# Outputs and statistics by batch element, and other rearrangements, in a four-layer decoder kernel

## Chip, cores and metric

The kernel runs on one core of one Trainium2 chip. The metric is the device time of one launch in microseconds (us), the median of several runs. The engines are TensorE (PE, its weight loads PEld), VectorE (DVE), ScalarE (ACT), GpSimd (POOL) and SyncE (SP), which issues most DMAs.

## The reference

Two sequences of 512 tokens with 128 features pass twelve residual stages, each on its layer norm:

```python
for f in (L0_attn, L0_xattn, L0_ffn, L1_attn, L1_xattn, L1_ffn,
          L2_attn, L2_xattn, L2_ffn, L3_attn, L3_xattn, L3_ffn):
    x = x + f(layernorm(x), ...)
```

The parts that matter here:

- `L0_attn` and `L1_attn` are causal attentions of 16 heads, `L2_attn` is a full one; each ends in an output projection, `out = o @ Wo`.
- `L1_xattn` takes its queries from x, and its keys and values from x and from a context of 77 tokens, with 2 heads.
- `L2_xattn` and `L3_xattn` are cross attentions of 16 narrow heads (8 features each) onto the 77 context tokens. `L2_xattn` clips its scores to 10000, and an output whose softmax sums are not numbers is replaced by an average.
- `L2_ffn` is a mixture of 16 experts with an RMS norm of its own, which has a weight: `xn = xf / rms * norm_weight; logits = xn @ router_weight.T + router_bias`. Each expert takes its 64 best tokens, `xe = xn[idx]`.

## The kernel before

The whole activation `m.x` stays in SBUF as 8 tiles of 128 tokens: tiles 0 to 3 are batch element 0 ("half 0"), 4 to 7 are element 1 ("half 1"). Each stage (l0a, l0x, l0f, l1a, l1x, l1f, l2a, l2x, l2f, l3a, l3x, l3f) has a function for every engine. Each engine issues its instructions in the order in which they are written, stage after stage, with semaphore waits between the engines.

**PSUM banks.** There are eight. A named result (`item`) has a bank: `fill` makes TensorE wait until all earlier results of that bank have been taken out, `read` makes a reader wait until the result is there, `copied` until it is taken out. `pair` and `run` in `plan` give bank 6 to the even numbers of a list and bank 7 to the odd ones. So `l1xo0`, `l1xy0`, `l2ao0`, `l2ay0` are in bank 6, and `l1xo1`, `l1xy1`, `l2ao1`, `l2ay1` in bank 7. In l2x the small results `l2xg0` and `l2xh0` are in bank 6, and so is `l2xy0`. The attention results of l0a and l1a are in bank 7.

**End of an attention stage.** TensorE writes x (the identity times x, `x_tensor`, one matmul of 128x512 a half) into the two y banks and adds the output projection (`tokens_tensor` or `sums_tensor`, four token tiles a half; in l1a four terms a tile). A float32 matmul shows as two instructions in the trace. VectorE takes the statistics of each half from the bank (`moments_of_sums`, `half_moments`: bn_stats, bn_aggr, variance). GpSimd makes the root (`norm_gpsimd`), ScalarE copies the new x out (`take_x`), VectorE normalises each half (`norm_to_turn`), TensorE turns it (`turn_tensor`), and ScalarE copies the turned tokens (`turn_scalar`, L223). Meanwhile TensorE issues fillers, matmuls of the identity with itself whose result nobody reads (`busy_through_norm`): so many, a wait for both variances, so many, a wait for the first root, so many. The attention result gets into `o_t` through GpSimd in l0a and l1a (`quad_scaled` counts its halves or groups), through ScalarE in l1x and l2a, through VectorE in l2x and l3x. At the start of l3f, GpSimd clears two buffers after l3x's statistics and before it makes the roots.

**The narrow loops** (l2x and l3x, `narrow_cross` and `narrow_vector`). There are 16 steps: batch element, query tile, half of the heads. TensorE issues in step k the scores of step k (L1950, into banks 0 and 1 or 2 and 3); the transposes of step k-3 (L1964, into banks 4 and 5), which wait for the exponential and for ScalarE's copy of the transposes before (`cross_taken`); and in every second step, for steps k-6 and k-5 together, the values (L1977) and the sums (L1982) into one bank. VectorE does in step k, in l2x, clip and maximum, in l3x maximum and subtraction; and in every second step, a step after TensorE's sums, the reciprocal group (L1901 and following: reciprocal of the sums, output times it, in l2x also a sum over the reciprocals). In l2x GpSimd subtracts the maximum (L2080). ScalarE does the exponential of step k (L897) and the copy of the transposes of step k-2 (L913).

**l2f's norm.** VectorE makes (x - mean) times the norm weight, a row repeated on all partitions, and then multiplies by the root. TensorE turns the tiles, ScalarE copies them. After the routing a matmul gathers the chosen tokens and ScalarE copies them (`chosen_t`, L2226).

Of the kernel before, what the change touches and what calls it, by code (L numbers as in the profile page):

```python
# [598 lines left out]
def l0_attn_tensor(nc, pe, m):  # L599
# [43 lines left out]
    x_tensor(nc, pe, m, "l0y")  # L643
    pe.wait_ge(m.quad_scaled, B)
    tokens_tensor(nc, pe, m, "l0y", m.o_t, w["wo"], on_x=True)


# [7 lines left out]
def x_tensor(nc, pe, m, name):  # L655


    for j in range(2):
        bank = fill(m, pe, f"{name}{j}")
        nc.tensor.matmul(bank[:, :], m.ident[:, :], m.x[:, 4 * j:4 * j + 4, :].rearrange("p t d -> p (t d)"), start=True,  # L660
                         stop=False, skip_group_check=True)


def tokens_tensor(nc, pe, m, name, x_t, w, on_x=False):
    sums_tensor(nc, pe, m, name, [(lambda t: x_t[:, t * P:(t + 1) * P], w)], on_x)


def sums_tensor(nc, pe, m, name, pairs, on_x):

    for j in range(2):  # L670
# [8 lines left out]
def project_out_tensor(nc, pe, m, source, name, w):  # L679

    x_tensor(nc, pe, m, name)
    for j in range(2):
        copied(m, pe, f"{source}{j}")
    tokens_tensor(nc, pe, m, name, m.o_t, w, on_x=True)
# [688 lines left out]
def l1_attn_tensor(nc, pe, m):  # L1373
# [51 lines left out]
    def q_ready(pe, b, j, qt):  # L1425
        group = GROUP * b + j
        if qt == 0 and group >= EARLY:
# [10 lines left out]
    x_tensor(nc, pe, m, "l1az")  # L1438
    pe.wait_ge(m.quad_scaled, B + 2 * GROUP)
    sums_tensor(nc, pe, m, "l1az", [(lambda t, r=r: m.wide[:, r, t * P:(t + 1) * P], m.lat_out[:, r * P:(r + 1) * P])  # L1440
                                    for r in range(GROUP)], on_x=True)

# [80 lines left out]
def l1_cross_tensor(nc, pe, m):  # L1523
# [34 lines left out]
    for k in range(XSTEPS + 3):  # L1558
# [20 lines left out]
        if j >= 0 and (j + 1) % (2 * NQ) == 0:  # L1579
            b = j // (2 * NQ)  # L1580
            pe.wait_ge(m.cross_taken, x0 + j + 1)
# [13 lines left out]
    project_out_tensor(nc, pe, m, "l1xo", "l1xy", w["wo"])  # L1595


def l1_cross_scalar(nc, act, m):
# [46 lines left out]
    copy_out_scalar(nc, act, m, "l1xo", m.o_t)  # L1645
# [156 lines left out]
def l2_attn_tensor(nc, pe, m):  # L1802
# [29 lines left out]
    project_out_tensor(nc, pe, m, "l2ao", "l2ay", w["wo"])  # L1832
# [44 lines left out]
def narrow_vector(nc, dve, m, a, stage):  # L1877
# [3 lines left out]
    for k in range(XSTEPS + 6):  # L1881
# [14 lines left out]
        n = k - 6  # L1896
# [10 lines left out]
def narrow_cross(stage, clip=None):  # L1907
# [8 lines left out]
    def tensor(nc, pe, m):  # L1916
# [24 lines left out]
        for k in range(XSTEPS + 5):  # L1941
# [26 lines left out]
            if n >= 0 and n % 2 == 1:  # L1968
# [6 lines left out]
                for j in range(GROUP):  # L1975
                    for g in range(GROUP):
                        nc.tensor.matmul(bank[own(g), 0:P], m.values_own[0:SC, b, g, j, :],  # L1977
                                         m.xpt[0:SC, g % 2, g // 2 * GROUP + j, qt * P:(qt + 1) * P], start=j == 0, stop=False,
                                         skip_group_check=True)
                for j in range(GROUP):  # L1980
# [5 lines left out]
        if clip:  # L1986
# [11 lines left out]
            keep_busy(nc, m, 7, 0)  # L1998
            pe.wait_ge(m.sums_are_numbers, 3)
        x_tensor(nc, pe, m, f"{stage}y")  # L2000
        copied(m, pe, f"{stage}o{B * NQ - 2}")
        copied(m, pe, f"{stage}o{B * NQ - 1}")
        tokens_tensor(nc, pe, m, f"{stage}y", m.o_t, w["wo"], on_x=True)
# [207 lines left out]
def l2_ffn_scalar(nc, act, m):  # L2211
# [3 lines left out]
    turn_scalar(nc, act, m, "l2fn")  # L2215
# [1611 lines left out]
```

## Time and profile before

| | |
|---|---|
| median of 3 runs | 1432.03 us (1428.06 to 1438.11) |
| profiled execution | 1430.51 us, its span 1428.7 us |
| mean granted TensorE clock | 0.979 |
| busy PE, DVE, ACT, POOL | 1333.0, 929.2, 671.9, 345.4 us |
| chain that ended last | PE 75%, DVE 11%, ACT 5%, DMA 4%, issue 3%, POOL 1% |
| first x product at the end of l0a, l1a, l1x, l2a | 136.50, 484.51, 566.71, 628.65 us |
| first x product at the end of l2x, l3x | 703.22, 911.23 us |

A time in the trace counts from the start of the span. In a timeline, a line is a run of like instructions: start us, length us from the first start to the last end, engine, line of the kernel, operation, output from inputs, form and count; in brackets the idle time of the engine before it and what ended that. A clock of 1.00 is 2.4 GHz, 0.50 is 1.2 GHz. Matmuls are pipelined, so that consecutive lines of TensorE can overlap by some 0.1 us.

### The profile page before, as it was taken

Reading aid. Unit: us, or ns where it says so; the run is one execution under the profiler, and the core shown is the slowest. Engines: PE = TensorE matmul, PEld = TensorE weight load, DVE = VectorE, ACT = ScalarE, POOL = GpSimd, SP = SyncE. Lnnn points to the kernel's source line nnn. Section 1 sums busy time; section 2 is a strip of 40 time slices with the busy share of each in tenths; the row PEclk is TensorE's granted clock in tenths of the full one; section 3 lists DMA queues with packets and bytes.
Section 4 is the critical chain, followed back from the end, with each engine's and each line's share of the span. In section 5 each row is a group of like instructions: output and inputs, shape, how many; then the busy total and the mean of one; then the engine's idle time right before and its main releaser. Section 6 shows DMA issues by size and latency. Waiting matters only on the chain.

```text
span 1428.7 us, 29436 instructions
## 1 busy us (share of the span) xinstructions
PE 1333.0 (93%) x11626; PEld 861.1 (60%) x11626; DVE 929.2 (65%) x1890; ACT 671.9 (47%) x1697; POOL 345.4 (24%) x373
## 2 busy tenths in 40 slices
PE   8998999999999889999989898899999999999986
PEld 6766565446666765667868586754435555654434
DVE  6776765343667555356684367588888876678755
ACT  5886533342787454344303245425557777740002
POOL 4000330001011100114203011177787465300001
PEclk9999999999999999999999989999999999999998
DMA  3000105100000000000124002101020110699980
GB/s 135 3 2 3 40 0 202 52 29 16 2 2 3 18 1 0 21 4 2 46 99 134 12 7 82 31 16 45 30 59 16 22 26 16 142 220 253 248 198 15
DMA packets 25352, 80.60 MB, mean 56 GB/s; under 512 B 5243, under 2 KB 7306, under 8 KB 24834
## 3 DMA queue, kind: packets, MB, share of 16 engines
q1 hardware_dynamic: 24354, 75.60, 19.4%
q10 hardware_dynamic: 864, 3.15, 0.8%
q8 instruction: 92, 1.51, 0.4%
q14 instruction: 42, 0.34, 0.1%
HBM read 72.17 MB, written 1.08 MB: 51 GB/s over the span
## 4 chain that ended last, share of the span: by engine, by line
PE 75%; DVE 11%; ACT 5%; DMA 4%; issue 3%; POOL 1%; SPq 0%; DVEq 0%; ACTq 0%; POOLq 0%
PE psum L2967 7%; PE psum L196 7%; PE psum L431 5%; PE psum L2988 5%; PE psum L2681 4%; PE psum L1267 4%; PE psum L2637 4%; PE psum L1261 3%; PE psum L451 3%; PE psum L2651 3%; PE psum L495 2%; PE psum L674 2%; DMA heads<-scratch_out_gates 2%; PE psum L2690 2%; DMA context_v<-scratch_out_gates 2%
## 5 line engine op out<-in xcount | busy, mean ns | idle before, releaser
L196 PE MATMUL psum<-ident 128*128 128x128 f32 x1272 | 159.6, 284 | 9.1 <-DMA ident<-in_ident 3.8
L187 POOL TENSOR_TENSOR rstd<-var,minus_half 128x4 f32<-128x4 f32 x30 | 31.3, 1043 | 557.9 <-DVE var L144 528.4
L196 PEld LDWEIGHTS psum<-ident 128*128 128x128 f32 x1272 | 153.2, 199 | 17.1 <-issue 7.7
L574 DVE TENSOR_REDUCE quad_max<-psum 128x1 f32<-128x128 f32 (+3 forms) x256 | 113.1, 484 | 55.8 <-PE psum L435 53.9
L529 ACT ACTIVATE pt<-psum,quad_max 128x128 f32<-128x128 f32 (+3 forms) x256 | 133.3, 530 | 26.7 <-DVE quad_max L574 26.6
L2988 PE MATMUL psum<-pt,slots 128*128 128x512 f32 x256 | 114.6, 599 | 5.0 <-DVE pt L3142 4.7
L2967 PE MATMUL psum<-slots,xn_t 128*128 128x512 f32 x256 | 113.9, 605 | 3.1 <-DVEq L3113 3.1
L2726 ACT ACTIVATE p<-psum,duo_max 128x512 f32<-128x512 f32 x128 | 86.8, 683 | 41.8 <-DVE duo_max L2761 41.7
L3057 ACT ACTIVATE pt<-psum,p 128x64 f32<-128x64 f32 x256 | 57.8, 392 | 72.7 <-POOL wide L3199 41.9
L2988 PEld LDWEIGHTS psum<-pt,slots 128*128 128x128 f32 x256 | 47.1, 189 | 71.7 <-issue 48.8
L2967 PEld LDWEIGHTS psum<-slots,xn_t 128*128 128x128 f32 x256 | 49.6, 194 | 66.0 <-issue 57.8
L2761 DVE TENSOR_REDUCE duo_max<-psum 128x1 f32<-128x512 f32 x128 | 82.3, 684 | 10.1 <-PE psum L2637 8.0
L2681 PEld LDWEIGHTS psum<-pt,wide 128*64 128x64 f32 x1024 | 54.6, 136 | 47.8 <-issue 25.0
L1349 DVE TENSOR_TENSOR pt<-pt,wide 128x512 f32<-128x512 f32 x64 | 43.0, 690 | 52.5 <-ACT pt L1296 43.0
L3130 DVE TENSOR_TENSOR pt<-psum,p 128x512 f32<-128x512 f32 x96 | 65.3, 686 | 17.8 <-PE psum L2967 13.5
L957 ACT ACTIVATE o_t<-psum 128x512 f32<-128x512 f32 x12 | 6.9, 596 | 142.7 <-PE psum L651 118.5
L2637 PE MATMUL psum<-heads 64*128 64x512 f32 x256 | 70.4, 630 | 3.2 <-ACT pt L3057 3.2
L2681 PE MATMUL psum<-pt,wide 128*64 128x128 f32 x1024 | 69.9, 279 | 1.1 <-ACT wide L2717 1.1
L451 PE MATMUL psum<-ident,pt 64*128 64x64 f32 x1280 | 63.8, 229 | 7.5 <-DVE pt L511 3.1
L1296 ACT ACTIVATE pt<-psum,slots 128x512 f32<-128x512 f32 x64 | 44.0, 687 | 56.5 <-PE psum L1261 56.3
L2709 DVE COPY pt<-psum 128x512 f32<-128x512 f32 x64 | 44.2, 691 | 40.0 <-PE psum L2651 39.4
L511 DVE COPY pt<-psum 128x256 f32<-128x256 f32 (+1 forms) x96 | 57.0, 593 | 10.7 <-PE psum L451 10.1
(515 smaller groups left out, 2796.8 us busy)
## 6 DMA issues: line engine op xcount, KB each, us to landing
pt<-scratch_out_gates SPq DMA_DIRECT2D x32, 256.0 KB, 12.9
heads<-scratch_out_gates SPq DMA_DIRECT2D x24, 256.0 KB, 15.6
slots<-in_s_l0f SPq DMA_DIRECT2D x8, 514.0 KB, 3.3
wide<-scratch_gates SPq DMA_DIRECT2D x8, 512.0 KB, 6.9
slots<-in_s_l3v SPq DMA_DIRECT2D x8, 512.0 KB, 3.7
context_v<-scratch_out_gates SPq DMA_DIRECT2D x16, 256.0 KB, 18.1
slots<-in_s_l3o ACTq DMA_DIRECT2D x6, 512.0 KB, 10.3
weights<-in_w_l1a SPq DMA_DIRECT2D x1, 2624.0 KB, 9.7
```

The lines of the kernel that those rows point to most:

```text
L196: nc.tensor.matmul(m.ps[bank][:, 0:P], m.ident[:, :], m.ident[:, :], start=True, stop=True, skip_group_check=True)
L431: nc.tensor.matmul(m.ps[g][:, 0:keys], q(g, b, j, qt), k(g, b, keys), start=True, stop=False)
L451: last = nc.tensor.transpose(banks[half][:, at:at + 64], m.quad_p[own, n % 2, g, kt * P:(kt + 1) * P], m.ident[own, own])
L529: nc.scalar.activation(m.quad_p[:, i % 2, g, 0:keys], m.ps[g][:, 0:keys], ACT.Exp, bias=m.quad_max[:, i % 2, g:g + 1], accum_out=sum_colum ...
L574: nc.vector.tensor_reduce(m.quad_max[:, n % 2, g:g + 1], m.ps[g][:, 0:keys], AX.X, ALU.max, negate=True).then_inc(m.quad_negmax, 1)
L2637: nc.tensor.matmul(m.ps[2 * (n % 2) + e], m.pair_rope[own, r % 2, 0, b * S + qt * P:b * S + (qt + 1) * P], m.pair_rope[own, r % 2, 1, b * ...
L2681: last = nc.tensor.matmul(m.ps[O_BANK][64 * e:64 * e + 64, qt * P:(qt + 1) * P], m.wide[:, r, at:at + 64], m.duo_pt[:, n % 2, e, kt * P:(k ...
L2726: nc.scalar.activation(m.p[:, 2 * (i % 2) + e, :], m.ps[2 * (i % 2) + e], ACT.Exp, bias=m.duo_max[:, i % 2, e:e + 1], accum_out=m.quad_sum ...
L2761: nc.vector.tensor_reduce(m.duo_max[:, n % 2, e:e + 1], m.ps[2 * (n % 2) + e], AX.X, ALU.max, negate=True).then_inc(m.duo_negmax, 1)
L2967: nc.tensor.matmul(m.ps[n % MIX_BANKS], m.xn_t[:, t * P:(t + 1) * P], m.slots[:, pair % 2, h * S:(h + 1) * S], start=True, stop=True).then ...
L2988: nc.tensor.matmul(m.ps[6 + b], m.slots[:, r % 2, e * P:(e + 1) * P], m.gated[:, k % 4, :], start=False, stop=False, skip_group_check=True ...
L3130: tt(by_feature(mixed[:, n % 4, :]), by_feature(m.ps[n % MIX_BANKS]), gate.rearrange("p (o e) -> p o e", o=1).broadcast_to([P, 64, E3]), A ...
```

## The change

- In l0a, l1a, l1x, l2a and l3x the x product and the projection are issued for half 0 and then for half 1, each behind its own wait. In l1x half 0 goes ahead of the attention values of batch element 1, and ScalarE copies the first half of `o_t` within its loop.
- In the loops of l2x and l3x the sums are issued one step after the values, behind that step's scores and transposes; VectorE's reciprocal group goes a step later too.
- At the end of l2x the x products take the place of the last seven fillers, ahead of the wait for VectorE's masked copy.
- In l2f the norm weight is a column and becomes the scale of ScalarE's copies of the turned and of the chosen tokens; VectorE normalises as in the other stages.

The diff, without most of its context lines:

```diff
@@ -640,9 +640,10 @@
     pe.wait_ge(m.quad_taken[T_BANKS.index(6)], a.turns_end[T_BANKS.index(6)])
-    x_tensor(nc, pe, m, "l0y")
-    pe.wait_ge(m.quad_scaled, B)
-    tokens_tensor(nc, pe, m, "l0y", m.o_t, w["wo"], on_x=True)
+    for j in range(2):
+        x_tensor(nc, pe, m, "l0y", (j,))
+        pe.wait_ge(m.quad_scaled, j + 1)
+        tokens_tensor(nc, pe, m, "l0y", m.o_t, w["wo"], on_x=True, halves=(j,))
@@ -652,22 +653,22 @@
-def x_tensor(nc, pe, m, name):
-    for j in range(2):
+def x_tensor(nc, pe, m, name, halves=range(2)):
+    for j in halves:
         bank = fill(m, pe, f"{name}{j}")
-def tokens_tensor(nc, pe, m, name, x_t, w, on_x=False):
-    sums_tensor(nc, pe, m, name, [(lambda t: x_t[:, t * P:(t + 1) * P], w)], on_x)
-def sums_tensor(nc, pe, m, name, pairs, on_x):
-    for j in range(2):
+def tokens_tensor(nc, pe, m, name, x_t, w, on_x=False, halves=range(2)):
+    sums_tensor(nc, pe, m, name, [(lambda t: x_t[:, t * P:(t + 1) * P], w)], on_x, halves)
+def sums_tensor(nc, pe, m, name, pairs, on_x, halves=range(2)):
+    for j in halves:
         bank = m.ps[m.items[f"{name}{j}"][0]] if on_x else fill(m, pe, f"{name}{j}")
@@ -676,12 +677,12 @@
-def project_out_tensor(nc, pe, m, source, name, w):
-    x_tensor(nc, pe, m, name)
-    for j in range(2):
-        copied(m, pe, f"{source}{j}")
-    tokens_tensor(nc, pe, m, name, m.o_t, w, on_x=True)
+def project_out_half(nc, pe, m, source, name, w, j):
+    x_tensor(nc, pe, m, name, (j,))
+    copied(m, pe, f"{source}{j}")
+    tokens_tensor(nc, pe, m, name, m.o_t, w, on_x=True, halves=(j,))
@@ -1435,10 +1436,11 @@
     pe.wait_ge(m.quad_taken[T_BANKS.index(6)], a.turns_end[T_BANKS.index(6)])
-    x_tensor(nc, pe, m, "l1az")
-    pe.wait_ge(m.quad_scaled, B + 2 * GROUP)
-    sums_tensor(nc, pe, m, "l1az", [(lambda t, r=r: m.wide[:, r, t * P:(t + 1) * P], m.lat_out[:, r * P:(r + 1) * P])
-                                    for r in range(GROUP)], on_x=True)
+    for j in range(2):
+        x_tensor(nc, pe, m, "l1az", (j,))
+        pe.wait_ge(m.quad_scaled, B + (j + 1) * GROUP)
+        sums_tensor(nc, pe, m, "l1az", [(lambda t, r=r: m.wide[:, r, t * P:(t + 1) * P], m.lat_out[:, r * P:(r + 1) * P])
+                                        for r in range(GROUP)], on_x=True, halves=(j,))
@@ -1578,6 +1580,8 @@
             b = j // (2 * NQ)
+            if b == 1:
+                project_out_half(nc, pe, m, "l1xo", "l1xy", w["wo"], 0)
             pe.wait_ge(m.cross_taken, x0 + j + 1)
@@ -1592,7 +1596,7 @@
             last.then_inc(filled(m, f"l1xo{b}"), 1)
-    project_out_tensor(nc, pe, m, "l1xo", "l1xy", w["wo"])
+    project_out_half(nc, pe, m, "l1xo", "l1xy", w["wo"], 1)
@@ -1642,7 +1646,10 @@
                                  turned_of(m, j).rearrange("p (b q) -> p b q", q=P), ACT.Copy).then_inc(m.cross_taken, 1)
-    copy_out_scalar(nc, act, m, "l1xo", m.o_t)
+        if k in (2 * NQ + 5, XSTEPS + 1):
+            b = 0 if k < XSTEPS else 1
+            bank = read(m, act, f"l1xo{b}")
+            nc.scalar.activation(m.o_t[:, b * S:(b + 1) * S], bank[:, :], ACT.Copy).then_inc(emptied(m, f"l1xo{b}"), 1)
@@ -1829,7 +1836,8 @@
     attend_tensor(nc, pe, m, None, a)
-    project_out_tensor(nc, pe, m, "l2ao", "l2ay", w["wo"])
+    for j in range(2):
+        project_out_half(nc, pe, m, "l2ao", "l2ay", w["wo"], j)
@@ -1878,7 +1886,7 @@
     nk, d = a.nk, m.dve
-    for k in range(XSTEPS + 6):
+    for k in range(XSTEPS + 7):
         if k < XSTEPS:
@@ -1893,7 +1901,7 @@
                 nc.vector.tensor_tensor(to, scores, spread, ALU.subtract).then_inc(m.negmax_ready, 1)
-        n = k - 6
+        n = k - 7
         if n >= 0 and n % 2 == 1:
@@ -1938,7 +1946,7 @@
         own = lambda g: slice(32 * g, 32 * g + 32)
-        for k in range(XSTEPS + 5):
+        for k in range(XSTEPS + 6):
             if k < XSTEPS:
@@ -1977,6 +1985,11 @@
                                          skip_group_check=True)
+            n = k - 6
+            if n >= 0 and n % 2 == 1:
+                b, _, qt = units[n]
+                name = f"{stage}o{n // 2}"
+                bank = m.ps[m.items[name][0]]
                 for j in range(GROUP):
@@ -1995,12 +2008,14 @@
                              stop=True).then_inc(filled(m, f"{stage}h0"), 1)
-            keep_busy(nc, m, 7, 0)
+            x_tensor(nc, pe, m, f"{stage}y")
             pe.wait_ge(m.sums_are_numbers, 3)
-        x_tensor(nc, pe, m, f"{stage}y")
-        copied(m, pe, f"{stage}o{B * NQ - 2}")
-        copied(m, pe, f"{stage}o{B * NQ - 1}")
-        tokens_tensor(nc, pe, m, f"{stage}y", m.o_t, w["wo"], on_x=True)
+            tokens_tensor(nc, pe, m, f"{stage}y", m.o_t, w["wo"], on_x=True)
+        else:
+            for j in range(2):
+                x_tensor(nc, pe, m, f"{stage}y", (j,))
+                copied(m, pe, f"{stage}o{B * NQ - 2 + j}")
+                tokens_tensor(nc, pe, m, f"{stage}y", m.o_t, w["wo"], on_x=True, halves=(j,))
@@ -2212,7 +2227,7 @@
     take_x(nc, act, m, "l2xy", 11)
-    turn_scalar(nc, act, m, "l2fn")
+    turn_scalar(nc, act, m, "l2fn", scale=w["norm_w"])
     bank = read(m, act, "l2fr0")
@@ -2223,7 +2238,8 @@
         bank = read(m, act, f"l2fx{j}")
-        nc.scalar.activation(m.chosen_t[:, j * S:(j + 1) * S], bank, ACT.Copy).then_inc(emptied(m, f"l2fx{j}"), 1)
+        nc.scalar.activation(m.chosen_t[:, j * S:(j + 1) * S], bank, ACT.Copy, scale=w["norm_w"]).then_inc(
+            emptied(m, f"l2fx{j}"), 1)
@@ -2245,16 +2261,7 @@
     dve.wait_ge(m.loaded["l2f"], 16)
-    for j in range(2):
-        copied(m, dve, f"l2xy{j}")
-        last = less_mean_times(nc, m, lambda t: m.x[:, t, :], w["norm_w"], j)
-    d.done(last)
-    for j in range(2):
-        root_of_half(dve, m)
-        for t in range(4 * j, 4 * j + 4):
-            last = nc.vector.tensor_scalar(m.xn[:, t, :], m.xn[:, t, :], m.rstd[:, t:t + 1], None, ALU.mult)
-        last.then_inc(m.xn_ready, 1)
-    m.turns_dve += 2
+    norm_to_turn(nc, dve, m, sums="l2xy")
@@ -3721,7 +3728,7 @@
                     ("router_b", column(np.tile(np.pad(v["L2_ffn_router_bias"], (0, 32 - E2)), 4))),
-                    ("norm_w", every(v["L2_ffn_norm_weight"])),
+                    ("norm_w", v["L2_ffn_norm_weight"].reshape(P, 1)),
                     ("one_to_cap", every(np.arange(1, CAP + 1, dtype=np.float32)))]
```

## Rows read from the trace of the kernel before

**Rows 1.** Timeline of TensorE, end of l0a.

```profile
136.50 1.88 PE L660 MATMUL psum<-x,ident 128*128 128x512 f32 x4
138.78 2.05 PE L674 MATMUL psum<-weights,o_t 128*128 128x128 f32 x16 [0.41 <-POOL o_t L561]
```

**Rows 2.** Timelines of TensorE and VectorE, end of l1a.

```profile
493.48 5.75 PE L196 MATMUL psum<-ident 128*128 128x128 f32 x50
...
495.26 2.38 DVE L161 TENSOR_SCALAR xn<-x,moments,rstd 128x128 f32<-128x128 f32 x8
```

**Rows 3.** Timelines of TensorE and ScalarE, end of l1x.

```profile
562.26 3.65 PE L1588 MATMUL psum<-pt,v 128*64 128x512 f32 x16 [0.69 <-ACT pt L1643]
...
566.71 1.98 PE L660 MATMUL psum<-x,ident 128*128 128x512 f32 x4
...
576.37 0.66 PE L215 MATMUL psum<-ident,xn 128*128 128x128 f32 x4 [0.37 <-DVE xn L161]
...
566.82 0.60 ACT L957 ACTIVATE o_t<-psum 128x512 f32<-128x512 f32 x1 [4.12 <-PE psum L1591]
```

**Rows 4.** Timeline of TensorE, end of l2a.

```profile
628.65 1.02 PE L660 MATMUL psum<-x,ident 128*128 128x512 f32 x2
629.98 1.12 PE L660 MATMUL psum<-x,ident 128*128 128x512 f32 x2 [0.30 <-ACT o_t L1854]
```

**Rows 5.** Chain in order of time, loop of l2x: start, length, what.

```profile
677.09 0.77 PE psum L1964 x16
677.86 1.01 PE psum L1977 x32
678.87 0.87 PE psum L1982 x32
679.74 0.74 PE psum L1950 x4
...
682.14 0.88 DVE k_t L1901
```

**Rows 6.** Windows, loop of l2x: busy PE, PEld, DVE, ACT, POOL; clock.

```profile
670.30:677.10 6.80, 6.74 (x90) 5.06 (x82) 3.19 (x5) 2.73 (x4) 1.69 (x2) 0.50 0.01 2
...
682.50:688.10 5.60, 3.91 (x100) 3.36 (x100) 4.54 (x8) 3.26 (x5) 2.44 (x3) 1.00 0.01 3
```

**Rows 7.** Timeline of TensorE, loop of l2x, transposes.

```profile
669.37 0.77 PE L1964 MATMUL psum<-ident,p 64*77 64x64 f32 x16 [1.59 <-ACT pt L913]
...
688.28 0.77 PE L1964 MATMUL psum<-ident,p 64*77 64x64 f32 x16 [1.69 <-ACT pt L913]
```

**Rows 8.** Timelines of TensorE and VectorE, end of l2x.

```profile
703.22 1.98 PE L660 MATMUL psum<-x,ident 128*128 128x512 f32 x4
...
701.81 1.35 DVE L2058 COPY_PREDICATED o_t<-number,average 128x512 f32<-128x512 uint32 x2
```

**Rows 9.** Timeline of TensorE, start of l2f, fillers.

```profile
706.82 6.86 PE L196 MATMUL psum<-ident 128*128 128x128 f32 x60
```

**Rows 10.** Line L223 on ScalarE by form: count, min/median/max ns.

```profile
L223 ACT ACTIVATE xn_t<-psum x24: 592/597/598, 11.5 to 1401.6; 128x512 f32<-128x512 f32 x24
L223 ACT ACTIVATE xn_t<-psum,weights x4: 682/729/777, 146.1 to 500.4; 128x512 f32<-128x512 f32 x4
```

**Rows 11.** Timeline of TensorE, loop and end of l3x.

```profile
876.79 0.77 PE L1964 MATMUL psum<-ident,p 64*77 64x64 f32 x16 [0.63 <-ACT pt L913]
...
902.35 0.77 PE L1964 MATMUL psum<-ident,p 64*77 64x64 f32 x16 [1.20 <-ACT pt L913]
...
912.70 1.12 PE L660 MATMUL psum<-x,ident 128*128 128x512 f32 x2 [0.35 <-DVE o_t L1902]
```

**Rows 12.** Chain in order of time, loop and end of l3x.

```profile
885.27 0.56 PE psum L1964 x16
...
914.75 0.90 DVE stats L134 x4
...
917.60 0.96 POOL v L3175
```

## The prediction

> **What bounds the kernel now.** I read the page first. TensorE carries 75% of the chain that ended last (the table of the profile above), so a change pays only where it shortens TensorE's own order of work, or where TensorE stands idle. The change touches six stage ends and two loops. For each I read the timeline of TensorE, to see its idle time and what ended it; then the timelines of VectorE, ScalarE and GpSimd; then the chain in order of time. The reader is to see that the ends differ. Some have short idle gaps on TensorE; at the end of l1a fillers run on after the result that they bridge to is there [rows 2]. In the two narrow loops TensorE waits in every pair of steps for ScalarE's copy, itself the end of a chain in l2x and alone in l3x [rows 7, 11].
>
> **Unit costs.** An x product of one half (identity times x) is half of the 1.88 us row: 0.94. The eight matmul instructions of one half's projection are about 0.9: sixteen end 2.05 after the start, pipeline fill included [rows 1]. VectorE's statistics take 1.4 us a half: both halves run from 914.75 to just before 917.60 [rows 12].
>
> **End of l0a.** Now: both x products, an idle 0.41 for GpSimd's second scaling, then sixteen projection instructions up to 140.83 [rows 1]. Changed: x0 to 137.44, projection 0 to 138.33, x1 to 139.27. The scaling is over by 138.78, so projection 1 ends near 140.2. The weight folds queued behind it on TensorE start 0.6 earlier. VectorE's and GpSimd's earlier statistics lie beside these folds and give nothing more. Gain 0.6 (0.3 to 0.7).
>
> **End of l1a.** The wait for the scaling is over long before the sums, and the same TensorE work follows in another order. The second half's sums end when they did. Behind them stand 25 fillers (50 instructions) from 493.48 to 499.2, while the normalised tokens are ready at 497.64 [rows 2]. First statistics that come 1 us earlier meet fillers that run by count. Gain 0 (up to 0.2).
>
> **End of l1x.** The first half's x product and projection (0.94 + 0.9) move ahead of the second values, into the 0.69 us in which TensorE waits for ScalarE. So the values start at 563.3 and not at 562.26, and end 1.05 later, at 567.8. Their consumer, ScalarE's copy, also comes 1.05 later. Now the trap: the second output's bank, 7, is also that of the second attention result (both lists alternate 6 and 7). The x product of half 1 must therefore wait for this copy of 0.60, which today ends under the x product of half 0 [rows 3]. It starts at about 568.5, takes 1.1 after an idle wait, and projection 1 ends at 570.5, as today. The old gap is filled and a new one of the same size appears. What is left: today statistics 1 queue 0.5 behind statistics 0 (1.4, begun when half 0's projection ends, 0.9 before half 1's); this queue goes. Behind the projection 22 fillers run by count; only the 0.37 us wait ahead of the second turn goes [rows 3]. Gain 0.3 (0 to 1.1, the latter without the trap). ScalarE's first o_t copy moves into the loop, where ScalarE waits for VectorE's maxima; that covers it. If that cover were gone, it would cost its own 0.60 [rows 3].
>
> **End of l2a.** Today x1 starts at 629.98, after 0.30 idle for the copy of the second attention result [rows 4]. Changed: x0 to 629.6, projection 0 to 630.5, and x1 starts there, the copy being over. Projection 1 ends at 632.35 instead of 632.88. Gain 0.5 (0.3 to 0.6).
>
> **The loop of l2x.** A step pair in full clock takes 11.19 / 2 = 5.6 us: 677.09 to 688.28 is four steps [rows 5, 7]. The chain through these four: transposes, values 1.01, sums 0.87, scores 0.74 on TensorE, VectorE's clip and maximum, the reciprocal group (0.88 and on, about 1.4), clip and maximum again, GpSimd, exponential, copy, transposes. The change takes both the sums (0.87) and the reciprocal group (1.4) out of this chain, each behind the next scores. Without them it would be 8.9 for four steps, 4.5 a pair. But VectorE's own work of a pair is 4.54 [rows 6], and its order, with the copy-before-transposes rule of a single pair of banks, leaves some waiting. I take halfway between 5.6 and 4.6: 5.1 a pair, over six pairs (0.5 each): 2.9 (0.5 to 6). The result bank is not reused for three more steps, so neither the fill of that bank nor the in-order reciprocal waits for anything new.
>
> One stretch of this loop ran at 0.50 granted clock, that is 1.2 GHz, from 670.3 to 677.1, right after an idle 1.59 us on TensorE. The pair there took 7.72 instead of 5.6 (669.37 to 677.09), so it costs 2.1 [rows 5 to 7]. With shorter waits I expect no such stretch here: 2.1 more (0 to 2.1). The Trainium skill ("TensorE: Matmul & The Clock Gate", Part 1) says that the gate looks at activity without regard to where a kernel starts, so that the same kernel differs from run to run. By that, the runs of before need not all have had this stretch here and the 2.1 would be partly noise; the trace of one execution cannot show it.
>
> **End of l2x.** Seven fillers give way to the x products, which then need not run behind the masked copy. Today the x products begin at 703.22. Changed: bank 6 is free only when VectorE has read the last small result in it, just before the masked copy starts at 701.81. So x0 starts near 701.9, x1 ends near 703.9, after the masked copy (703.16) [rows 8]. The projection starts 1.3 earlier than at 705.2. Gain 1.3 (1.2 to 1.8).
>
> **Norm weights in l2f.** VectorE loses eight scalar-tensor-tensor instructions and eight multiplies and gets eight fused ones. But TensorE runs 30 fillers (60 instructions, 6.86 us) by count in this interval [rows 9], and their number isn't changed, so VectorE's saving stays hidden. What costs is ScalarE's copy with a column of weights as scale: 729 ns against 597 [rows 10]. Of four such copies two end on the path: loss 0.2 (0 to 0.5). The Trainium skill ("ScalarE: Activation LUTs", What ACT_TABLE_LOAD costs) puts each such operand at about 93 ns; the row says 132, and the difference would be under 0.1 us in all. The smaller weight load ends ahead of need either way.
>
> **The loop of l3x.** Here TensorE waits 0.63 a pair for ScalarE's copy of the transposes just done. Five pairs take 25.56 us, 5.11 each [rows 11]. The chain of a pair: transposes 0.77, values 1.01, sums 0.87, scores 0.74 as in l2x [rows 5], second transposes 0.56 [rows 12], and the remaining 1.16 is the copy with its hand-overs. After the change sums and scores lie between the second transposes and the next ones, and they cover the copy. The pair becomes TensorE's own work: 0.56 + 1.01 + 0.74 + 0.56 + 1.0 (sums, now after transposes like the values) + 0.74 = 4.6. Gain 0.5 a pair, 2.6 for five; in the tail, where the wait is 1.20 [rows 11], 0.9 more. Gain 3.5 (1 to 4.3).
>
> **End of l3x.** x1 waits until 912.70 for VectorE's last o_t [rows 11], with projection 0 queued behind. Changed: projection 0 comes first and x1 starts at 913.1. Projection 1 ends 0.7 earlier; statistics 1 no longer queue behind statistics 0: 1.15 earlier. GpSimd's two memsets (from 917.60), the roots and the normalising all hang on that [rows 12], and here the fillers end before the roots. Gain 1.15 (0.7 to 1.4).
>
> **Sum.** 0.6 + 0 + 0.3 + 0.5 + 2.9 + 2.1 + 1.3 - 0.2 + 3.5 + 1.15 = 12.15. The profiled execution took 1430.51 (span 1428.7), 1.5 under the median of the runs, 1432.03. So 1418.4 for it and 1420 for the median, 0.8% less. A measurement of this kernel tells about 1% from no change, and three runs of before lie 10 us apart.
>
> **Rivals.** (A) The loops keep their pace where VectorE and GpSimd set it: l2x gives nothing, and its half-clock stretch stays; the rest stands. 12.15 - 2.9 - 2.1 = 7.2, so 1425. For it: VectorE has 4.54 of work in 5.6. Against: both removed terms lie in the chain itself. (B) The loops reach their floors: l2x at VectorE's 4.6 a pair (6.0 instead of 2.9), l3x without the extra 0.14 of sums after transposes (+0.8), and one more of the other half-clock stretches falls away (2.1). 12.15 + 6.0 = 18.2, so 1414. (C) The change does not do what it says: in-order engines hold the earlier halves back in both loops and ends, and only the replaced fillers and the end of l3x pay: 2.5, so 1430. Against it stand the named gaps. (D) Slower: TensorE's order with shorter matmul runs drops the clock inside the loops. A pair at half clock takes 7.7 [rows 5, 7] instead of 4.6 or 5.1. Four pairs at half clock cancel everything; all six of l3x make 18.6 of loss, 1439. Against: in l3x's loop with 0.63 us gaps the clock never fell, and the gaps shrink.
>
> **How the numbers follow.** Forecast 0.42, A 0.22, B 0.26, C 0.06, D 0.04. The range goes from 1411, below B with what run noise adds, to 1429, above A. Faster by over 1% (below 1417.7): B and the lower edge of the forecast, 0.36. Slower 0.03. Within 1%: 0.61.
>
> **What would show it.** L1982 a step after L1977; transposes of l3x's loop without idle time before them and 4.6 us a pair; l2x near 5.1 and at full clock; at the end of l1x an idle gap ahead of the second x product; the end of l1a and the l2f fillers unchanged in length; l3x's memsets 1.1 earlier relative to its last sums. I am wrong if transposes still wait in l3x, if the clock falls in either loop, or if half-clock stretches elsewhere outweigh all of it.

## The result, and the profile after

The changed kernel takes 1418.83 us (median of 7 runs, 1414.98 to 1423.37), the kernel before 1432.03 (also 7 runs, 1428.06 to 1438.11). The ratio is 0.991, with a 95% interval of 0.9888 to 0.9932: faster by 0.9%. The profiled execution took 1418.38 us (span 1416.6), against 1430.51 (span 1428.7): 12.1 less. I take the stages in the order of the prediction.

End of l0a, timeline of TensorE (start, length, engine, line, operation, idle time before it):

```profile
136.91 1.02 PE L661 MATMUL psum<-x,ident 128*128 128x512 f32 x2
137.77 1.05 PE L675 MATMUL psum<-weights,o_t 128*128 128x128 f32 x8
138.66 1.02 PE L661 MATMUL psum<-x,ident 128*128 128x512 f32 x2
139.52 1.05 PE L675 MATMUL psum<-weights,o_t 128*128 128x128 f32 x8
140.50 0.67 PE L1015 MATMUL psum<-keys_own,weights 64*128 64x156 f32 x6
```

The idle 0.41 ahead of the projection [rows 1] is gone. From the last transposes of the attention to the first weight fold it takes 4.03 us in place of 4.71. The end of l1a is unchanged (8.97 before and 8.96 after, from the first x product to the fillers).

End of l1x, the same view, and behind it a row of ScalarE's timeline:

```profile
561.96 1.02 PE L661 MATMUL psum<-x,ident 128*128 128x512 f32 x2
562.83 1.05 PE L675 MATMUL psum<-weights,o_t 128*128 128x128 f32 x8
563.81 3.65 PE L1592 MATMUL psum<-pt,v 128*64 128x512 f32 x16
...
569.02 1.12 PE L661 MATMUL psum<-x,ident 128*128 128x512 f32 x2 [0.70 <-ACT o_t L1652]
...
568.37 0.60 ACT L1652 ACTIVATE o_t<-psum 128x512 f32<-128x512 f32 x1 [5.61 <-PE psum L1595]
```

The first half fills the old wait of 0.69 ahead of the values [rows 3]. A new wait of 0.70 stands ahead of the second x product: it starts when ScalarE has emptied the bank. From the last transposes of l1x to l1f's own x product ("the end of l1x") it takes 15.21 us in place of 15.57. At the end of l2a the second x product starts at 630.63 without a wait; from the attention's last values to l2x's first product it takes 8.14 in place of 8.72.

Loop of l2x, from the chain in order of time (start, length, what):

```profile
675.42 0.77 PE psum L1972 x16
676.19 1.01 PE psum L1995 x32
677.20 0.74 PE psum L1958 x4
...
677.97 0.81 DVE p L1897
...
678.80 0.80 DVE xmax L1899
679.60 0.88 DVE k_t L1909
```

The sums (L1995, before L1982) now follow transposes, with no values in between. The reciprocal (k_t) still stands in the chain, between two pairs of VectorE's instructions. Four steps of this chain take 10.31 us (transposes at 665.11 to transposes at 675.42), before 11.19: what left it is one run of 0.87 on TensorE, not the group. The six pairs took 5.11, 6.07, 7.72, 5.60, 5.59 and 5.64 before, and 4.59, 5.00, 5.32, 4.99, 4.96 and 5.82 after.

The two loops as windows (start and end; length; busy time of PE, PEld, DVE, ACT, POOL; granted clock; DMA share; GB/s):

```profile
657.90:692.90 35.00, 33.09 (x774) 26.48 (x773) 24.81 (x40) 20.17 (x24) 13.26 (x13) 1.00 0.01 4
870.40:901.20 30.80, 29.99 (x756) 24.89 (x756) 23.25 (x34) 20.48 (x24) 0.00 (x0) 1.00 0.02 3
```

Both ran at clock 1.00 throughout, that is at 2.4 GHz, and TensorE is busy 95% and 97% of them. From the transposes ahead of the first values to the product behind the last sums, the loop of l2x takes 35.01 us in place of 40.06.

End of l2x and start of l2f, timelines of VectorE and TensorE:

```profile
696.42 1.34 DVE L2073 COPY_PREDICATED o_t<-number,average 128x512 f32<-128x512 uint32 x2
696.45 1.98 PE L661 MATMUL psum<-x,ident 128*128 128x512 f32 x4 [0.25 <-DVE number L2068]
698.27 1.95 PE L675 MATMUL psum<-weights,o_t 128*128 128x128 f32 x16
...
700.05 6.86 PE L196 MATMUL psum<-ident 128*128 128x128 f32 x60
...
702.35 2.38 DVE L161 TENSOR_SCALAR xn<-x,moments,rstd 128x128 f32<-128x128 f32 x8
```

The x products start beside the masked copy, when VectorE has read the last small result, and not behind it [rows 8]. The projection starts 5.41 us after the loop, before 6.79. In l2f the normalised tokens are ready at 704.73, but the fillers run until 706.75, as long as they did [rows 9]. From the projection to the router's matmul it takes 10.48 us, before 10.34.

Loop and end of l3x, the chain first, then timelines of TensorE and GpSimd:

```profile
872.85 0.54 PE psum L1972 x16
873.39 1.01 PE psum L1995 x32
874.40 0.72 PE psum L1958 x4
875.12 0.54 PE psum L1972 x16
875.66 1.01 PE psum L1985 x32
876.67 0.72 PE psum L1958 x4
```

```profile
901.25 1.13 PE L661 MATMUL psum<-x,ident 128*128 128x512 f32 x2
902.21 1.05 PE L675 MATMUL psum<-weights,o_t 128*128 128x128 f32 x8
...
906.49 0.96 POOL L3182 MEMSET v<- 128x1024 f32 x1 [48.43 <-DVEq L3637]
...
909.36 1.16 PE L196 MATMUL psum<-ident 128*128 128x128 f32 x8 [0.33 <-POOL rstd L187]
```

A pair is 4.54 us of TensorE's own work: two transposes, values, sums and two score groups, without the 0.63 of waiting [rows 11]. In the tail, where waits of 1.20 and 1.21 stood, transposes still wait 0.19, 0.43 and 0.19. The loop with its tail takes 30.90 us in place of 34.44 (from transposes at 870.35 to the x product at 901.25; before from the like ones to 911.23). From there to l3f's first product it takes 11.78 in place of 12.91.

The ledger: 0.68 + 0 + 0.36 + 0.58 + 5.05 + 1.38 - 0.14 + 3.54 + 1.13 = 12.58 us, against 12.1 less span. The six ends and the norm make 4.0 of it. Over the profiled kernels that share an end's code and run it at full clock, its length repeats within 0.05 us.

### The profile page after: what moved, and what is told of

Read it like the earlier page. It is cut to its first block, busy times and chain, and to the rows that moved or that the text cites. A ratio compares the mean times of both kernels' runs of the same rounds, so it can differ in the third digit from the quotient of the medians.

```text
span 1416.6 us, 29395 instructions
## 1 busy us (share of the span) xinstructions
PE 1330.0 (94%) x11612; PEld 860.1 (61%) x11612; DVE 927.6 (65%) x1882; ACT 672.1 (47%) x1697; POOL 344.6 (24%) x373
## 4 chain that ended last, share of the span: by engine, by line
PE 76%; DVE 11%; ACT 5%; DMA 4%; issue 3%; POOL 1%; SPq 0%; DVEq 0%; ACTq 0%; POOLq 0%
PE psum L2974 7%; PE psum L196 7%; PE psum L431 5%; PE psum L2995 5%; PE psum L2688 4%; PE psum L1268 4%; PE psum L2644 4%; PE psum L1262 3%; PE psum L451 3%; PE psum L2658 3%; PE psum L495 2%; PE psum L675 2%; PE psum L2697 2%; DMA heads<-scratch_out_gates 2%; DMA context_v<-scratch_out_gates 2%
## 5 line engine op out<-in xcount | busy, mean ns | idle before, releaser
L2995 PE MATMUL psum<-pt,slots 128*128 128x512 f32 x256 | 114.4, 598 | 4.7 <-DVE pt L3149 4.2
L2995 PEld LDWEIGHTS psum<-pt,slots 128*128 128x128 f32 x256 | 47.2, 189 | 71.1 <-issue 49.4
L2688 PEld LDWEIGHTS psum<-pt,wide 128*64 128x64 f32 x1024 | 54.6, 136 | 48.2 <-issue 24.3
```

The lines of the kernel that those rows point to most:

```text
L2688: last = nc.tensor.matmul(m.ps[O_BANK][64 * e:64 * e + 64, qt * P:(qt + 1) * P], m.wide[:, r, at:at + 64], m.duo_pt[:, n % 2, e, kt * P:(k ...
L2995: nc.tensor.matmul(m.ps[6 + b], m.slots[:, r % 2, e * P:(e + 1) * P], m.gated[:, k % 4, :], start=False, stop=False, skip_group_check=True ...
```

## The experiments

In each diff, "-" is the changed kernel and "+" the experiment, if not said otherwise. Kernels without a number of runs ran once, and their totals say little beside their stages: 1420.34 us (sums late only), 1427.09 (group late only), 1421.95 (own bank), 1420.23 (fewer fillers), 1413.19 (old norm, fewer fillers). Own bank and fewer fillers even came out above the changed kernel; both had 54.6 us at half clock ahead of the last 30, the changed kernel's profiled execution 47.8.

**The loops alone.** The kernel before, with only the sums and the reciprocal group a step later in the narrow crosses:

```
-    for k in range(XSTEPS + 6):        (VectorE)
+    for k in range(XSTEPS + 7):
-        n = k - 6
+        n = k - 7
-        for k in range(XSTEPS + 5):    (TensorE)
+        for k in range(XSTEPS + 6):
     ... the sums' matmuls moved under: n = k - 6; if n >= 0 and n % 2 == 1
```

> Only the later sums and the later reciprocal group, in both narrow loops, on the kernel before. My theory: from the first combined transposes on, l2x's loop takes 5.0 us less and l3x's 3.5 us less than before, all other stages take what they took; so 1430.5 - 8.5 = 1422 for the profiled execution, a ratio near 0.994. l3x's loop at 4.54 us a step pair without idle time before the transposes. Rival (the stage ends carry the gain): the loops give under 4 us together and the total stays above 1426.

Measured: 1420.66 us (6 runs), ratio 0.9927 (0.99 to 0.9955). l2x's loop took 35.01 and l3x's 30.9, as in the changed kernel; all ends kept their old times. In whole times the ends don't show clear of noise: 1418.83 us with them, 1420.66 without, and the intervals overlap. Their 4.0 us rest on the stages.

**All but the loops.** The changed kernel with the loops of before:

> The changed kernel with both narrow loops as they were. My theory: the stage ends give 0.7 (l0a), 0 (l1a), 0.4 (l1x), 0.6 (l2a), 1.4 (l2x), -0.1 (l2f) and 1.1 (l3x), 4 us together: 1426.5, ratio 0.997. Step pairs of 5.6 us in l2x and 5.11 in l3x. If the half-clock stretch in l2x's loop belongs to its idle time, it is there again; if it came there by the phase of the run alone, it is as likely elsewhere.

Measured: 1431.99 us (12 runs), ratio 0.9991 (0.9968 to 1.0014). The ends gained as in the changed kernel (l0a 4.07, l1x 15.22, l2a 8.14, l2x 5.42), but l3x's end took 12.95: a half-clock stretch from the loop reaches 2.4 us into it. And the loops lost: 42.93 and 36.6 us, against 40.06 and 34.44 before. The window in l2x's loop and the last of l3x, both at about half clock:

```profile
683.00:697.00 14.00, 12.80 (x156) 10.76 (x144) 4.39 (x8) 4.38 (x5) 3.54 (x5) 0.51 0.01 1
...
908.00:915.00 7.00, 7.00 (x101) 5.59 (x94) 2.50 (x4) 0.04 (x1) 0.00 (x0) 0.52 0.01 2
```

The expected 1426.5 us missed by 5.5. In this execution the ends' 2.8 us are in their stages, and the two loops, with their half-clock stretches, lost 5.0; this profiled execution (1432.81) lies 2.3 above the one before. This is one execution; that it also explains the median of twelve is argued, not shown. In its favour: the granted clock averages 0.979 over these runs and over the 39 runs of the kernel before that went with the timed experiments, and 0.984 for the loops alone.

**Which half of the loop edit.** Two kernels, each with one of its two moves: the sums on TensorE, or VectorE's reciprocal group.

```
sums late only                            group late only
-    for k in range(XSTEPS + 7):          -        for k in range(XSTEPS + 6):
+    for k in range(XSTEPS + 6):          +        for k in range(XSTEPS + 5):
-        n = k - 7                        and the sums' matmuls back under n = k - 5
+        n = k - 6
```

> TensorE's sums a step later as in the changed kernel, VectorE's reciprocal group back in its old step. My theory: l3x's loop, which waited for ScalarE's copy alone, keeps nearly all of its gain on TensorE's side, unless VectorE, which now must wait for sums that are issued in the same step behind the transposes, holds up the next maximum; VectorE then stands about 1 us a pair and the loop takes 4.6 to 5.2 a pair. In l2x, where VectorE is in the chain, the pair is slower than in the changed kernel's 5.1: 5.4 or more. Rival (moving the sums is all that counts): both loops as in the changed kernel.

> TensorE's sums back in their old step, VectorE's reciprocal group a step later. My theory: l3x's loop is back at 5.11 a pair, as its chain holds no VectorE work; in l2x the group (1.4) leaves the chain of four steps and the sums (0.87) stay: 11.19 - 1.4 = 9.8 for four steps, 4.9 to 5.3 a pair, against 5.6 before and 5.1 changed. Rival (both moves are needed together in l2x as well): 5.6 a pair.

Measured, sums alone: l3x 30.66 us with pairs of 4.54; l2x 35.61, 5.2 a pair on average and not the 5.4 or more of my theory. The old step of VectorE's group holds nothing up in l3x and costs 0.6 in all in l2x. Group alone: l2x 35.52 in pairs of 5.11, l3x in pairs of 5.11 as before, both as expected. TensorE's timeline in l3x, and a window of its tail, which ran at half clock, so that this loop took 37.36 us:

```profile
878.59 0.77 PE L1972 MATMUL psum<-ident,p 64*77 64x64 f32 x16 [0.63 <-ACT pt L914]
```

```profile
899.00:910.00 11.00, 11.00 (x147) 9.12 (x144) 2.94 (x7) 1.02 (x1) 0.00 (x0) 0.53 0.01 3
```

The wait of 0.63 is there again. In l3x only the place of the sums counts: they cover ScalarE's copy. In l2x either move takes some 2.4 us out of 38 (40.06 less the half-clock excess), and both together 3.0. The chain of l2x with the group alone tells why they don't add:

```profile
665.10 0.56 PE psum L1972 x16
...
665.68 1.03 ACT pt L914
...
666.84 0.77 PE psum L1972 x16
```

VectorE has left this chain. What is left is TensorE's work and the uncovered copy, as in l3x before, with the same 5.11 a pair. With the sums alone the copy is covered, but VectorE and its group stay in the chain. With both moves VectorE's group stands in the chain again, for the mean pair of 5.11. So the two kernels with the group late reach the same pair in l2x by two different limits.

**A bank of its own.** The second output product of l1x goes to bank 0, not to bank 7, which it shares with the second attention result:

```
+    if name == "l1xy1":
+        return m.ps[0]
     ... and the same bank wherever this result is read or added to
```

> The changed kernel with one edit: the x and weight products of l1xy1 go to bank 0, so they share no bank with l1xo1. Theory (the shared bank 7 made the second x product wait for ScalarE's copy): the 0.70 us wait before the second x product goes, TensorE runs the two x products, the first weight fold and the second without a gap but for the wait on ScalarE's copy of o_t ahead of the second weight products, and from the last transposes of l1x to the x product of l1f it takes between 14.5 (the whole 0.7 gained) and 15.2 us. Rival (the second weight products need the same copy a microsecond later, so the wait only moves behind the x product): the idle time shows there instead and the stage keeps its 15.21 us. By the rows, the copy ended when the second x product started, so after it the weight products find it done: I expect the gain, about 0.7 us. All other stages unchanged; the whole 1418.4 less 0.7 or so, within what one run can tell.

Measured, TensorE and ScalarE at the end of l1x:

```profile
569.02 1.03 PE L1601 MATMUL psum<-wide,context_v 77*64 77x512 f32 x4
...
569.98 1.12 PE L667 MATMUL psum<-x,ident 128*128 128x512 f32 x2
...
570.10 0.60 ACT L1658 ACTIVATE o_t<-psum 128x512 f32<-128x512 f32 x1 [5.61 <-PE psum L1601]
```

No wait is left on TensorE: the copy runs beside the x product. The end takes 14.45 us in place of 15.21, 0.76 less. The shared bank was the trap.

**Fewer fillers, with the new norm and with the old.** Three kernels: the fillers cut; the old two-step norm of l2f with the old fillers; the old norm with fewer fillers.

```
-    busy_through_norm(nc, pe, m, 6, 13, 8)          (into l1x)
+    busy_through_norm(nc, pe, m, 6, 13, 2, 3)
-    busy_through_norm(nc, pe, m, 11, 12, 8, 10)     (l2f)
+    busy_through_norm(nc, pe, m, 11, 12, 8, 1)
```

> The changed kernel with fewer of TensorE's counted 128-column filler matmuls under two norms: in l1x the last group 8 and 4 down to 2 and 3, in l2f 10 down to 1. Theory (behind the l2f norm VectorE ends 2.0 us ahead of the fillers, 704.73 against 706.75, and behind l1x's the fillers also run past the norm): the stretch from l2's projection to the router's matmul falls from 10.48 to about 8.5 us, l1x's end from 15.21 to about 13.8 us. Rival (the fillers hold nothing, another engine ends last): both keep their times and a wait shows in place of the fillers. A further risk: the granted clock falls to 0.50 in the stage behind, which would cost 3 to 7 us there.

> The changed kernel with the old VectorE norm of l2f (product with the weight row, then the product with the root) and plain ScalarE copies, everything else as changed. Theory (the saving on VectorE is hidden behind 60 filler matmuls and only the dearer scale copy shows): from the projection to the router's matmul 10.34 us, 0.13 less than the 10.48 of the changed kernel; whole 1418.3. Rival (the norm edit gave the gain that it was meant to and something else took it): 11 to 12 us here.

> The same old norm of l2f with the fewer filler matmuls of fewer_fillers. Theory: without the fillers' cover VectorE's two-step norm ends last in l2f, and the stretch from the projection to the router's matmul comes out at 9.7 us, against 8.5 with the new norm and the same fillers: so the norm edit is worth 1.2 us only if the fillers are cut with it. Rival (ScalarE's turn and copies set the end in both): both within 0.2 us of each other.

Measured from l2's projection to the router's matmul:

| | 30 fillers | 21 fillers |
|---|---|---|
| old norm | 10.35 | 9.46 |
| new norm (the change) | 10.48 | 8.47 |

The last waits, TensorE in the old norm with fewer fillers, and below it VectorE and TensorE with the new:

```profile
699.71 1.44 PE L215 MATMUL psum<-ident,xn 128*128 128x128 f32 x8 [0.56 <-DVE xn L2270]
```

```profile
703.91 2.38 DVE L161 TENSOR_SCALAR xn<-x,moments,rstd 128x128 f32<-128x128 f32 x8
...
706.30 1.04 PE L215 MATMUL psum<-ident,xn 128*128 128x128 f32 x8
```

So the new norm costs 0.13 us behind 30 fillers and saves 1.0 behind 21. The other cut lies ahead of l1x, between l1a's x product and l1x's turn (14.55 to 12.99); I had written "l1x's end", and the end stayed at 15.22. The granted clock was 1.00 in both shortened stretches. No run here shows how few fillers it would bear.

**The old norm, timed.** Its one execution above had taken 1413.59 us, 5.2 less than the changed kernel's median.

> The changed kernel with the old VectorE norm of l2f again, now timed. Its one execution took 1413.6 us, 5.2 less than the changed kernel, while its stages differ by only 0.13 us; the difference lay in where the half-clock stretches fell. If that was chance between executions (theory): median 1418 to 1419, ratio to the kernel before 0.991. If the old norm really is 5 us faster (rival): median 1413 to 1414, ratio 0.987.

Measured: 1416.93 us (6 runs, 1407.95 to 1421.48), ratio 0.9898 (0.9865 to 0.9932). It can't be told from the changed kernel's 0.991; the stages say 0.13 us. The first execution had 41 us at half clock ahead of its last 30, the profiled one of these six 47.8, with the very same code.

**GpSimd's roots first.** In l3f two memsets stood ahead of the roots:

```
     pool.wait_ge(m.stage_done, 11)
+    norm_gpsimd(nc, pool, m)
     for what in range(2):
         nc.gpsimd.memset(duo_turned_raw(m, what), 0.0).then_inc(m.turned_zero, 1)
-    norm_gpsimd(nc, pool, m)
```

> The changed kernel with GpSimd's two roots of l3f's norm put before its two memsets. Theory (with the statistics 1.8 us earlier, GpSimd's memsets at 906.49 and 907.39 now stand between the statistics and the roots; the roots start at 908.30): the roots run when the statistics come, the wait of 0.33 us for the roots and the one of 0.37 us for VectorE's norm go, and from the first x product after l3x's loop to l3f's first product it takes 10.7 us in place of 11.78, set now by the counted fillers. Rival (the memsets' readers, the DMA that fills the zeroed tiles, come late instead): this stretch is 10.7 us too, but the stage behind it grows by the same 1.1 us.

Measured: l3x's end took 11.03 us, not 10.7. The rows, in VectorE's and GpSimd's order:

```profile
904.99 2.04 POOL L187 TENSOR_TENSOR rstd<-var,minus_half 128x4 f32<-128x4 f32 x2 [48.45 <-DVEq L3637]
...
906.14 3.19 DVE L161 TENSOR_SCALAR xn<-x,moments,rstd 128x128 f32<-128x128 f32 x8 [1.09 <-POOL rstd L187]
906.92 0.97 POOL L3183 MEMSET v<- 128x1024 f32 x1
907.84 1.09 POOL L3183 MEMSET o_t<- 128x1024 f32 x1
```

Counted from the first x product, the roots start at 5.25 us and not at 7.05, but VectorE's norm beside the memsets takes 3.19 us for what takes 2.14 alone. The eight instructions of this norm by form (count, min/median/max ns), which ran beside the memsets:

```profile
L161 DVE TENSOR_SCALAR xn<-x,moments,rstd x8: 328/606/1065, 906.1 to 909.0; 128x128 f32<-128x128 f32 x8
```

**All together.** Roots first, own bank, fewer fillers, and 6 fillers fewer in l3f:

> The changed kernel with the roots first, the second y product of l1x in a bank of its own, the fewer filler matmuls of fewer_fillers, and none of the 6 between statistics and roots in l3f. If the stages add up: 0.76 (bank) + 1.56 (into l1x) + 2.0 (l2f) + about 2.3 (l3x's end, 9.5 us in place of 11.78) = 6.6 us less than the changed kernel, 1412 us, ratio to the kernel before 0.986. Rival (each cut shifts where the half-clock stretches fall, and these take 3.4 us each): every stage shows its gain, yet the whole lands anywhere in 1409 to 1419, and the median of several runs moves by less than 4 us against the changed kernel's 1418.8.

Measured: 1410.96 us (6 runs, 1404.99 to 1414.66), ratio 0.9864 (0.9833 to 0.9894). The expected 1412 was met by luck in part: the stages gave 5.1 us and not 6.6, and the rest of the 7.9 below the changed kernel came with a higher mean granted clock (0.986 against 0.982 over the runs). The expectation's 3.4 us for each half-clock stretch is no price that the traces show: stretches are 3.4 to 13.7 us long, and the pair in 6.8 us of it cost 2.1. Bank, l1x and l2f gave 0.76, 1.57 and 2.0; l3x's end came out at 11.04, not 9.5, since VectorE's norm set it: 898.55 to 901.74, again 3.19. Both roots had also waited, for the end of the stage before.

**Roots ahead of that wait.**

```
-    pool.wait_ge(m.stage_done, 11)
     norm_gpsimd(nc, pool, m)
+    pool.wait_ge(m.stage_done, 11)
```

> As combined, but GpSimd's two roots of l3f's norm stand before its wait for the end of the stage before, which came with the last statistics and held both roots until 897.41 there although the first statistics were ready at 895.72. Theory: the first root starts with the first statistics and the second at the second, VectorE scales the first half 1.7 us earlier and ahead of the memsets, only its second half runs beside a memset, and l3x's end falls from 11.04 to about 9.4 us. Rival (GpSimd's memset beside VectorE's norm, which took 3.19 us there against 2.14 us without it, costs as much in this order too): 10.5 us or more. The whole: 1411 less 1.6, 1409 us, ratio to the kernel before 0.985, within the spread that the half-clock stretches give.

Measured: l3x's end 10.03 us; 1411.69 us (6 runs, 1400.49 to 1417.2), ratio 0.9865 (0.9826 to 0.9905). The first root came with the first statistics, and VectorE's norm followed its statistics without a pause:

```profile
898.60 1.01 POOL L193 TENSOR_TENSOR rstd<-var,minus_half 128x4 f32<-128x4 f32 x1 [46.82 <-DVE var L150]
...
900.35 3.19 DVE L167 TENSOR_SCALAR xn<-x,moments,rstd 128x128 f32<-128x128 f32 x8
```

It still takes 3.19. So 1.0 of the 1.6 us came, and the rival's price, 1.05 us beside the memsets, stayed. Every run of the kernel with all together lies below every run of the changed kernel. With the roots ahead of the wait the ratio is as low, but its interval overlaps that of the changed kernel. Between the two the runs don't tell.

## Why the prediction was right

The forecast was 1420 us in a range of 1411 to 1429, and 1418.4 for the profiled execution; 1418.83 and 1418.38 came. Term by term, predicted and found:

| term | predicted | found | what showed it |
|---|---|---|---|
| end of l0a | 0.6 | 0.68 | idle 0.41 gone |
| end of l1a | 0 | 0 | fillers by count |
| end of l1x | 0.3 | 0.36 | own bank: 0.76 more |
| end of l2a | 0.5 | 0.58 | no wait at 630.63 |
| loop of l2x | 2.9 + 2.1 | 5.05 | loops alone: 5.05 |
| end of l2x | 1.3 | 1.38 | x product at 696.45 |
| norm of l2f | -0.2 | -0.14 | old norm: 0.13 back |
| loop of l3x | 3.5 | 3.54 | pair 4.54 |
| end of l3x | 1.15 | 1.13 | memsets still follow statistics |

The reasons held where an experiment tried them: the second result's bank 7, which makes its x product wait for the copy, the fillers that hide VectorE's saving, the copy in l3x that the sums cover. Rival A (the loops keep their pace) would have been 1425: the l2x loop fell by 2.9 without its half-clock stretch. Rival B (floors reached) needed 4.6 a pair in l2x; it stayed near 5.1. Rivals C and D fell with the same rows.

One term was right in its size and wrong in its parts. For l2x I took sums (0.87) and reciprocal group (1.4) out of one chain, which left 8.9 us for four steps, and put the value halfway between the old pace and the floor. The measured chain takes 10.31: only 0.87 left it, and the group is still in it. I also had no second limit behind the first: once VectorE is out, ScalarE's uncovered copy holds the pair at 5.11. The halfway value was a guess that fell well; the experiments, not the working, justify it. As this term is the second largest of the sum, the close hit of the total is luck to that extent. And the doubt after the result, that l3x might need VectorE's late group, was settled: the sums' place does it alone.

One price was misread, to little effect. The 729 ns of [rows 10] is the median of four copies in two forms: two of l0x with a column as scale took 687 and 682 ns, two of l1x with columns as scale and as bias 777 and 771. l2f's new copies, with a scale alone, took 687 and 680, some 87 more than 597 and not 132.

In l3x too the parts differ from the sum. Four pairs gave 2.2 us, the fifth with its tail wait 0.9, and the sixth 0.4, where I had 2.6 and 0.9.

The 2.1 for the half-clock stretch was the least certain term. It held in the sense that none of the eleven profiled kernels with the sums moved has a stretch in either loop, while the three with the sums in their old place (the one before, all but the loops, and group alone) have four between them, from 6.8 to 13.7 us long, each just behind idle times of 1.2 to 1.6 us ahead of transposes. That they go with the old place of the sums is what these 14 executions show; that the idle times bring them is argued. Against it: in the kernel before, an idle 1.69 us ahead of 688.28 in l2x and 1.20 ahead of 902.35 in l3x [rows 7, 11] brought no such stretch. The Trainium skill ("TensorE: Matmul & The Clock Gate", Part 1) says that the gate isn't aligned to where a kernel starts, so that stretches move between executions. The traces agree: two executions of one kernel, the old norm's, have 41 and 47.8 us at half clock ahead of their last 30.

The missing 0.5 us of the ledger lies outside the changed stages. Without the loop's stretch, the kernel before had 44.4 us at half clock ahead of its last 30 and the changed one 47.8; that this is the 0.5 is likely, not shown.

## What to carry to other kernels

Before you shorten an engine's work, look at what bridges it: here counted fillers hid 1 us of VectorE's saving until their number was cut with it. When an earlier half is issued ahead of a later one, list the banks both use, since the wait that you fill can come back as a wait for a bank. In a loop where an engine waits a fixed time for another's copy, put independent work of its own between the two, and before you add up two moves, ask what limits the loop once the first is made: in l2x another limit stood close behind, and two moves of 2.4 us each gave 3.0.

## What the runs showed of the hardware

**GpSimd's memset stops VectorE.** A VectorE tensor_scalar of 128x128 f32 takes 341 to 347 ns in l3f's norm of the changed kernel and up to 1065 with a GpSimd memset (0.97 to 1.09 us) beside it; the stretch of eight grows by 1.05 us, about one memset. The Trainium skill ("SBUF — State Buffer", Who interferes with whom) describes the ports that VectorE and GpSimd share as an exclusive lock held for a whole instruction; the longest of the eight fits one memset's length. A larger memset makes it plainer. It stands beside the norm at l1a's start, before and after the change; here the changed kernel's rows of GpSimd, and of VectorE by form:

```profile
342.62 3.51 POOL L1504 MEMSET heads<- 128x4096 f32 x1
...
L161 DVE TENSOR_SCALAR xn<-x,moments,rstd x8: 328/341/3506, 341.5 to 346.4; 128x128 f32<-128x128 f32 x8
```

One instruction took 3506 ns, as long as the memset, and this norm 5.32 us; TensorE had other work meanwhile. GpSimd's roots (1.0 to 1.1 us each) did not do this: in l3f of the changed kernel the instructions beside one kept their 341 to 347 ns.

**The transfer rate of the last stage differs between executions.** At the end of l3f TensorE's gated combination (L2995) hangs on VectorE, and VectorE on rows streamed from DRAM. Windows of the changed kernel, then of the kernel with the roots first, in the same part of that stream (last column GB/s):

```profile
1313.00:1338.00 25.00, 25.00 (x60) 11.03 (x59) 19.50 (x29) 0.00 (x0) 0.00 (x0) 1.00 1.04 254
1338.00:1363.00 25.00, 21.13 (x45) 7.30 (x43) 13.06 (x22) 0.00 (x0) 0.00 (x0) 1.00 1.04 248
```

```profile
1310.80:1335.80 25.00, 25.00 (x59) 11.02 (x58) 20.18 (x30) 0.00 (x0) 0.00 (x0) 1.00 1.03 305
```

At 305 GB/s TensorE never waited. At 254 and less the stream's buffers ran dry:

```profile
PE psum L2995 <- DVE pt L3149: 4.2, 12, 1.6
```

That is 4.2 us of TensorE's waiting, in 12 waits. Over the fourteen profiled kernels it was 4.2 to 6.2 us in twelve (about 250 GB/s), 2.2 in one (about 262) and 0 in this one, which took 1407.63 us. None of the edits touches this stream, and the kernel with all together, which has the same edit as this one, streamed at about 250 again. It is a second source of the spread of about 10 us between runs, beside the half-clock stretches, and the reason why the stages were compared here, and not single times.
